# A graph network kernel: batch 0's GAT stage and the edge tables put between the steps of layer 0's last chunk, score broadcasts made by transposes, and a new order of steps

## The reference

```python
def _L1_gnn_ref(h, adj_matrix, W, a):          # the "GAT" layer
    Wh = jnp.einsum('bnf,fo->bno', h, W)
    a1, a2 = (a[:Fout, 0], a[Fout:, 0])
    s1 = Wh @ a1
    s2 = Wh @ a2
    e = s1[:, :, None] + s2[:, None, :]
    e = jnp.where(e >= 0, e, ALPHA * e)
    e = jnp.where(adj_matrix[None] == 0, -jnp.inf, e)
    attention = jax.nn.softmax(e, axis=-1)
    h_prime = jnp.einsum('bij,bjo->bio', attention, Wh)
    return h_prime
...
    h = jnp.maximum(_layernorm(x, axis=-1), 0.0)
    x = x + _L0_gnn_ref(h, adj, ...)            # 8 Euler steps: h + dt*(0.5*alpha*(adj@h - h) + h@w_eff - h + x0)
    h = jnp.maximum(_layernorm(x, axis=-1), 0.0)
    x = x + _L1_gnn_ref(h, adj, ...)
    h = jnp.maximum(_layernorm(x, axis=-1), 0.0)
    x = x + _L2_gnn_ref(h, ..., adj, src, dst)  # attention over 256 edges, 4 heads: leaky_relu(Xq[src] + Xq[dst]) . a,
                                                # + log(adj[src, dst]), softmax by source node, sum of values, W_out
    h = jnp.maximum(_layernorm(x, axis=-1), 0.0)
    x = x + _L3_gnn_ref(h, adj, adj, ...)       # Chebyshev step with 2L/lambda_max - I, masked attention of 4 heads, FFN
```

## Time and profile before

| | us |
|---|---|
| median of 3 runs | 1332.32 (1326.53, 1332.32, 1336.32) |
| the profiled execution, its own time | 1326.59 |
| its span in the profile | 1324.8 |
| mean granted clock of PE, share of full | 0.957 |
| PE busy | 1176.4 (89%) |
| DVE busy, ACT busy, POOL busy | 784.3 (59%), 762.5 (58%), 473.9 (36%) |
| 16 DMA engines, mean share, moved | 83.68 MB, 63 GB/s |

### The profile page before, as it was taken

How to read it: one execution, slowest core, us unless ns; L and a number is a source line. 1 busy time by engine, 2 the same in 40 slices (tenths; PEclk the granted TensorE clock), 3 DMA queues, 4 the chain that set the end, 5 groups by cost and what they waited for, 6 DMA issues and landing times. The chain is left out here.

```text
span 1324.8 us, 24887 instructions
## 1 busy us (share of the span) xinstructions
PE 1176.4 (89%) x7613; PEld 920.3 (69%) x7613; DVE 784.3 (59%) x2837; ACT 762.5 (58%) x1612; POOL 473.9 (36%) x578
## 2 busy tenths in 40 slices
PE   4979999999999547899999999999999999999763
PEld 3658878888889435677776777777777677766542
DVE  6623213213332234677888888888888888866652
ACT  4213324234211023487888788788888878885770
POOL 4203003003125022335346445644644654552423
PEclk7989999999999768999999999999999999998996
DMA  4001020020200100223323423432432342343311
GB/s 117 16 17 33 24 65 8 25 72 1 64 9 9 32 8 17 66 68 99 90 71 97 112 64 87 111 89 62 111 95 62 97 111 65 86 104 86 96 51 31
DMA packets 123748, 83.68 MB, mean 63 GB/s; under 512 B 13216, under 2 KB 106784, under 8 KB 123680
## 3 DMA queue, kind: packets, MB, share of 16 engines
q1 hardware_dynamic: 123680, 82.82, 23.8%
HBM read 28.25 MB, written 20.97 MB: 37 GB/s over the span
## 5 line engine op out<-in xcount | busy, mean ns | idle before, releaser
L1726 DVE CUSTOM_DVE_ANT_0 att_Ts<-bank,mask_att 128x512 f32<-128x512 f32 x256 | 173.5, 685 | 71.7 <-PE bank L1811 70.2
L1521 ACT ACTIVATE att_Es<-att_Ts,att_small 128x512 f32<-128x512 f32 x256 | 184.6, 721 | 39.0 <-DVE att_small L1726 38.1
L1951 PE MATMUL bank<-ident,att_Es 128*128 128x128 f32 x1024 | 157.2, 276 | 23.3 <-ACT att_PTs L1529 22.7
L1529 ACT COPY att_PTs<-bank 128x512 f32<-128x512 f32 x256 | 147.5, 576 | 32.1 <-PE bank L1951 31.3
L1951 PEld LDWEIGHTS bank<-ident,att_Es 128*128 128x128 f32 x1024 | 118.5, 142 | 67.3 <-issue 29.8
L1811 PE MATMUL bank<-K_parts,Q_parts 128*128 128x512 f32 x256 | 125.6, 500 | 9.0 <-DMA K_parts<-k_lo 8.8
L290 POOL TENSOR_SCALAR l_rs<-l_mv 128x4 f32<-128x4 f32 x16 | 6.9, 431 | 251.3 <-DVE l_mv L470 251.1
L1456 POOL TENSOR_SCALAR gat_Vs<-gat_Ts,gat_small 128x512 f32<-128x512 f32 x64 | 62.4, 989 | 54.4 <-DVE gat_small L1603 54.4
L484 DVE TENSOR_TENSOR P_row<-bank,l_bias 128x512 f32<-128x512 f32 x32 | 22.1, 691 | 99.2 <-PE bank L855 77.8
L845 PE MATMUL bank<-G,x0T 128*128 128x128 f32 x384 | 75.0, 277 | 1.2 <-DVE U2T L479 1.0
L845 PE MATMUL bank<-G,U1T 128*128 128x128 f32 x384 | 74.4, 275 | 0.0
(11 more groups left out here) (307 smaller groups left out, 3101.2 us busy)
## 6 DMA issues: line engine op xcount, KB each, us to landing
Q_parts<-q_hi SPq DMA_DIRECT2D x128, 64.0 KB, 2.0
Q_parts<-q_lo SPq DMA_DIRECT2D x128, 64.0 KB, 2.0
K_parts<-k_hi SPq DMA_DIRECT2D x128, 64.0 KB, 2.0
K_parts<-k_lo SPq DMA_DIRECT2D x128, 64.0 KB, 2.0
l_x<-in_x SPq DMA_DIRECT2D x16, 256.0 KB, 2.9
P2T<-in_x SPq DMA_DIRECT2D x16, 256.0 KB, 4.2
x_after_l<-P2T SPq DMA_DIRECT2D x16, 256.0 KB, 2.3
gat_xin<-x_after_l SPq DMA_DIRECT2D x16, 256.0 KB, 2.9
```

What stands on the lines that cost most here:

```text
L1521: nc.scalar.activation(att_E[:, j % RING_E, :], att_T[:, j % RING_T, :], ACT.Exp, scale=-1.0, bias=att_small[:, 0, j:j + 1], accum_out=att ...
L1529: nc.scalar.copy(att_PT[:, i // NT, :, cols(i % NT)], c2[:].rearrange("p (s q) -> p s q", q=P)).then_inc(sem("att_pt"), 1)
L1726: nc.vector.tensor_tensor_reduce(att_T[:, j % RING_T, :], [c0, c1][j % 2][:], k.mask_att[:, j % NT, :], -QK_SCALE, HUGE, ALU.add, ALU.min, ...
L1951: mm = nc.tensor.transpose(c2[:, cols(s)], att_E[:, i % RING_E, cols(s)], k.ident[:])
```

## The change

The GAT stage moves out of `build_layers` into functions of its own (`gat_stage`, `gat_memory`), whose semaphores are kept over the barrier. Both blocks use it. Batch 0's whole GAT stage is issued by the front block, between the steps of the last chunk: `with_gat(lev, t)` says on each engine what follows which step. `pick_adj` moves from behind the last level to (0,3), where it reads `edge_pick` itself; `pick_s` is gone. The loads of the edge lists move to the first chunk and `same_src`, `src_rows` to the second. On POOL `gat_rstd(0)` stands ahead of the `edge_pick` tables. The semaphore clear becomes 12 instructions.

In both blocks the score vectors are folded in elsewhere: `gat_wh` multiplies by `W1ga`, 130 columns, of which the last two are the scores; `gat_s1`, `gat_s1_out`, `gat_a2b` are gone, `gat_s2` becomes 4 transposes of a broadcast column. `gat_wh_out` is two copies, one per half. The destination's edge scores come from `edge_lcol`, which moves ahead, a small copy `edge_lc` on DVE, and 8 transposes of broadcast columns (`edge_lb0/1`) where 4 matmuls with `head_a` stood. The three order tables are new: in the loop `cheb_g` is ahead of `gat_turn`, `ffn_turn` ahead of `att_turn3`, and `store_out` last on SP.

```diff
@@ -89,37 +95,36 @@
-        gat_a = sb("gat_a", [P, 2])
-        gat_a2b = sb("gat_a2b", [P, P])
-        head_a = sb("head_a", [P, H, P])
+        W1ga = sb("w_W1ga", [P, D + 2])
+        W["W1g"] = W1ga[:, 0:D]
         head_a4 = sb("head_a4", [P, H])
...
+        k["gat"] = gat_memory(nc)
+        k["gat_steps"] = gat_stage(nc, k, kept_sem)
         build_front(nc, k)
...
+        def gat_wh_out(n, half):
+            ready(act, "gat_wh", n, half + 1, 2)
+            freed(act, "gat_pv", n)
+            nc.scalar.copy(WhA[:, 2 * half:2 * half + 2, :],
+                           [a1, a0][half][:, 0:2 * (D + 2)].rearrange("p (t d) -> p t d", d=D + 2)
+                           ).then_inc(sem("gat_whs"), 1)
...
+        def gat_wh(n):
+            ready(pe, "gat_hT", n)
+            freed(pe, "gat_eT", n, NT)
+            w = D + 2
+            for t in range(NT):
+                mm = nc.tensor.matmul([a1, a0][t // 2][:, t % 2 * w:t % 2 * w + w], hTA[:, cols(t)], k.W1ga[:],
+                                      start=True, stop=True)
+                if t % 2:
+                    mm.then_inc(sem("gat_wh"), 1)
+
+        def gat_s2(n):
+            ready(pe, "gat_whs", n, 2, 2)
+            for t in range(NT):
+                mm = nc.tensor.transpose(a1[:, cols(t)], wh2[:, t, :].broadcast_to([P, P]), k.ident[:])
+            mm.then_inc(sem("gat_s2"), 1)
+
...
+                if ch == 0:
+                    for dst, src in edge_loads:
+                        load(dst, src, "edge_loaded")
                 if ch == NCH - 1:
                     sp.wait_ge(sem("u_ready"), 2 * B)
-                    for dst, src in edge_loads:
-                        load(dst, src, "edge_loaded")
+                    for t in range(NT):
+                        sp.wait_ge(kept_sem(f"l0_stored{t}"), 16)
+                    gat["load_x"](0)
...
+            def edge_tables():
+                nc.gpsimd.iota(node_row[:], [[1, N]], base=0, channel_multiplier=0,
+                               allow_small_or_imprecise_dtypes=True).then_inc(sem("node_numbers"), 1)
+                pool.wait_ge(sem("edge_f"), 2)
+                pool.wait_ge(sem("node_numbers"), 2)
+                for e in range(ET):
+                    nc.gpsimd.tensor_scalar(k.same_src[:, e, :], edge_f[:, 0, :], edge_c[:, 0, e:e + 1], None,
+                                            ALU.is_equal).then_inc(sem("rows"), 1)
+                    nc.gpsimd.tensor_scalar(k.src_rows[:, e, :], node_row[:], edge_c[:, 0, e:e + 1], None,
+                                            ALU.is_equal).then_inc(sem("rows"), 1)
...
+                if ch == 1:
+                    edge_tables()
...
+            gat["gat_rstd"](0)
...
+            for half in range(2):
+                for t in range(NT):
+                    nc.gpsimd.tensor_scalar(k.edge_pick[:, t, half * E:half * E + E], edge_f[:, half, :],
+                                            node_col[:, t:t + 1], None, ALU.is_equal).then_inc(sem("pick"), 1)
...
+            for t in range(NT):
+                gat[f"gat_low{t}"](0)
+            pool.wait_ge(sem("adj_picked"), ET)
...
+                elif (lev, t) == (1, 0):
+                    gat["gat_hT"](0)
+                elif (lev, t) == (1, 1):
+                    gat["gat_wh_out0"](0)
+                    gat["gat_wh_out1"](0)
...
+                elif (lev, t) == (2, 0):
+                    for q in range(NT):
+                        gat[f"gat_exp{q}"](0)
+                elif (lev, t) == (2, 1):
+                    gat["gat_eT0"](0)
+                    gat["gat_eT1"](0)
+                elif (lev, t) == (2, 2):
+                    gat["gat_eT2"](0)
+                    gat["gat_eT3"](0)
...
-                    nc.vector.tensor_scalar(k.head_a[r, h, :], k.ones[r, :], acol[r, :], None, ALU.mult
-                                            ).then_inc(sem("head_a"), 1)
...
+                if (lev, t) == (0, 3):
+                    gat["gat_stats"](0)
+                    gat["gat_aggr"](0)
+                elif (lev, t) == (1, 0):
+                    gat["gat_apply"](0)
+                    edge_weights()
...
+                        if ch == NCH - 1:
+                            for q in range(NT):
+                                gat[f"gat_scores{q}"](0)
+                            gat["gat_row1"](0)
+                            gat["gat_row2"](0)
+                            gat["gat_row3"](0)
+            gat["gat_rinv"](0)
+            gat["gat_x2a"](0)
+            gat["gat_x2b"](0)
...
+                if (lev, t) == (0, 3):
+                    pick_adj()
+                elif (lev, t) == (1, 0):
+                    gat["gat_turn"](0)
+                elif (lev, t) == (1, 1):
+                    gat["gat_wh"](0)
...
+                elif (lev, t) == (2, 1):
+                    gat["gat_eturn0"](0)
+                    gat["gat_eturn1"](0)
+                elif (lev, t) == (2, 2):
+                    gat["gat_eturn2"](0)
+                    gat["gat_eturn3"](0)
+                elif (lev, t) == (2, 3):
+                    gat["gat_pv0"](0)
+                    gat["gat_pv1"](0)
...
             def pick_adj():
 
                 pe.wait_ge(sem("pick"), NT)
-                pe.wait_ge(sem("lap"), NT)
+                pe.wait_ge(sem("lap"), 2 * NT)
                 for e in range(ET):
                     for t in range(NT):
-                        mm = nc.tensor.matmul(bank[4 + e][:], pick_s[:, t, cols(e)], adj[:, t, :],
+                        mm = nc.tensor.matmul(bank[4 + e][:], k.edge_pick[:, t, cols(e)].bitcast(F32), adj[:, t, :],
                                               start=(t == 0), stop=(t == NT - 1))
                     mm.then_inc(sem("adj_picked"), 1)
...
-        cheb_prop0 cheb_prop1 att_turn1 att_score4 gat_turn cheb_g att_turn2 att_score5 gat_wh gat_s1 att_turn3
-        ffn_turn gat_s2 ffn_up0 att_score6 ffn_up1 att_turn4 att_score7 ffn_down0 ffn_down1 cheb_x1turn
...
+        cheb_prop0 cheb_prop1 att_turn1 att_score4 cheb_g gat_turn att_turn2 att_score5 gat_wh ffn_turn att_turn3
+        gat_s2 ffn_up0 att_score6 ffn_up1 att_turn4 att_score7 ffn_down0 ffn_down1 cheb_x1turn att_turn5 att_score8
+        edge_gather0 att_turn6 att_score9 edge_gather1 cheb_q edge_x att_turn7 att_score10 gat_eturn0 edge_lcol
+        att_turn8 edge_lb0 edge_lb1 att_score11 gat_eturn1 att_turn9 att_score12 cheb_k gat_eturn2 gat_eturn3 edge_v
...
-        load_x store_out+ load_ffn edge_store+ stack1+ stack3+ store_v+ load_v cheb_res stack0 stack2
+        load_x load_ffn stack1+ stack3+ store_v+ edge_store+ cheb_res load_v stack0 stack2 store_out
...
+            def edge_lc(n):
+                ready(dve, "edge_lcol", n)
+                freed(dve, "edge_lb", n, 2)
+                nc.vector.tensor_copy(edge_small[:, 5, :], b0[:, 0:ET * H]).then_inc(sem("edge_lc"), 1)
...
+            def edge_lcol(n):
                 ready(pe, "edge_z", n)
-                for h in (2 * q, 2 * q + 1):
-                    mm = one([b0, b1][q][:, (h % 2) * E:(h % 2) * E + E], k.head_a[:, h, :], zT[:])
-                mm.then_inc(sem("edge_lb"), 1)
-
-            def edge_lcol(n):
-                ready(pe, "edge_max", n, ET * H, ET * H)
                 for e in range(ET):
                     mm = one(b0[:, e * H:e * H + H], zT[:, cols(e)], k.head_a4[:])
                 mm.then_inc(sem("edge_lcol"), 1)
+
+            def edge_lb(n, q):
+                ready(pe, "edge_lc", n)
+                for h in (2 * q, 2 * q + 1):
+                    for e in range(ET):
+                        c = e * H + h
+                        mm = nc.tensor.transpose([b0, b1][q][:, (h % 2) * E + e * P:(h % 2) * E + (e + 1) * P],
+                                                 edge_small[:, 5, c:c + 1].broadcast_to([P, P]), k.ident[:])
+                mm.then_inc(sem("edge_lb"), 1)
```

767 lines of the change are left out of this document (396 added, 371 removed).

## The result

The changed kernel takes 1312.12 us (median of four runs, 1311.06 to 1314.35), the kernel before 1331.05 (four runs): a ratio of 0.986 with an interval of 0.983 to 0.990. It is faster by 1.4%, 19 us in the medians. I had said 1294, with a range of 1276 to 1311. Its profiled execution took 1312.6 us with a span of 1310.8, which is 14.0 us less than the span of before.

A forecast was written before the change was run, and what follows sets the result against it. PE was taken to bound the loop. Gains of 16 (front block), 1.3 (its start), 5 (fill), 15 (loop) and 1 (drain) sum to 38 us: 1326.6 becomes 1288.3, as a median 1294, range 1276 to 1311.

The forecast's parts named there:

- The stall ahead of `pick_adj`: Front block: PE waits 10.4 us for four `edge_pick` tables that POOL makes behind `gat_rstd(0)`.
- the early 1.3 us: Early front block: DVE's `gat_a2b` and `head_a` mostly go, so PE's wait for DVE's list shrinks by 1.3 us.
- The clears: Border between the blocks: 11 more semaphore clears on POOL cost 0.5 us, bounds 0 and 2.5.
- Rival 3: Front block: the GAT stage does not overlap and levels stretch; 16 us gain becomes 3, giving 1307; chance 0.08.
- the loop is bound by PE: Loop: PE, busy 45.36 of 47.30 us, sets the period; it shrinks by 1.5 us to 45.8, gaining 15 us.
- 0.81 + 0.5 + 1.0 = 2.3: Loop: PE work lost per iteration, 0.81 us from `gat_s1`, 0.5 from `gat_s2`, 1.0 from the edge scores.
- The floor under `ffn_turn`: Loop: `ffn_turn` needs POOL's `n2_b`, whose chain is not shortened, so it moves only 0.81 us ahead, not 1.28.
- Rival 2: Loop: removed matmuls turn into waits for DVE or ACT, the new order gives nothing; 1312 us; chance 0.14.
- The fill: Fill, batches 1 to 5: the same edits gain 5 us, bounds −2 and 10.
- The drain: Drain, with no GAT stage and one edge stage: 1 us gained.
- rival 5: DVE's `edge_lc` waits for `edge_lcol`, delaying masks, exponentials and PE's turns 4.5 us a round; 1354 us; chance 0.05.
- rival 4: The clock falls where transposes stand in a row, 3 us in each of 13 rounds; 1333 us; chance 0.03.

The follow-up runs named there:

- e1: The changed kernel with POOL's eight `edge_pick` tables ahead of `gat_rstd(0)`: 1295.82 us, ratio 0.973 to the kernel before.
- e2: The changed kernel with all kept semaphores taken first, so that one instruction clears the rest: 1305.65 us, ratio 0.982 to the kernel before.
- e16: The kernel before, unchanged, profiled a second time: 1328.09 us (one run).
- e14: The changed kernel with `cheb_k`'s matmul issued twice, 0.86 us more PE work per iteration: 1314.49 us, ratio 0.992 to the kernel before.
- e15: The changed kernel with `gat_wh`'s matmuls issued twice, 0.9 us more PE work per iteration: 1314.05 us, ratio 0.990 to the kernel before.
- e6: The changed kernel with `edge_lb` made again by four fp32 matmuls with `head_a`, in its new place: 1316.13 us, ratio 0.991 to the kernel before.
- e9: The changed kernel with the loop lists of before on PE, DVE, ACT, POOL and SP, adapted to the new operations: 1315.92 us, ratio 0.991 to the kernel before.
- e13: The changed kernel with POOL's `n2_b` adding the bias to the first of four node tiles only: 1307.74 us, ratio 0.985 to the kernel before.
- e7: The changed kernel with added matmuls that nobody reads at four PE waits in the fill: 1308.12 us, ratio 0.984 to the kernel before.
- e4: The changed kernel with `att_rv` back ahead of `cheb_aggr`, `ffn_final` and `gat_x2` in DVE's loop list: 1310.99 us, ratio 0.986 to the kernel before.
- e5: The changed kernel with the loop lists of before on PE, DVE, ACT and POOL, but SP's new list: 1350.12 us, ratio 1.017 to the kernel before.

## Why the prediction was wrong

**The front block: right in mechanism, one term too small.** 14.6 us came, 17.3 were forecast. The stall ahead of `pick_adj` (9.76 for 10.4), its second price in the clock (1.56 for 1.4), `gat_turn`'s wait (1.81 for 1.8) and the early 1.3 us (1.14: PE starts at 71.10 where it was at 72.24) are right, and e1 showed the stall to be POOL's order. The clears are the mis-sized term: 1.6 us (e2), for 0.5. Of the 2.7 us that are missing they are 1.1, and another 0.3 are at the border; 0.5 are that `pick_adj` starts at 406.96 and not at 407.8 − 1.3, and 0.8 lie between there and the x2 operations (61.7 us for 60.9). Rival 3, that the stage would not overlap, is out.

The two marks move with the granted clock as well. The stretch from 380 to 390 us, with PE at work in it, first before and then in the changed kernel:

```profile
380.00:390.00 10.00, 9.01 (x81) 8.93 (x81) 2.49 (x8) 0.62 (x1) 0.56 (x1) 1.00 0.15 28
380.00:390.00 10.00, 10.00 (x63) 10.00 (x62) 1.80 (x7) 0.62 (x1) 0.00 (x0) 0.66 0.01 2
```

So of the 1.14 us that PE was early at 71.10 only 0.4 are left where level 0 ends, at 397.0. The kernel before has such a dip in its second profile too (e16, 0.67), and there the first edge statistics come at 488.98 where the first profile had 488.07.

**The loop: the step that failed** is "the loop is bound by PE", read from PE's 96% share, and with it the sum "0.81 + 0.5 + 1.0 = 2.3" carried to the period. The period fell by 0.3 us. Adding 0.9 us of PE work did nothing (e14, e15), taking 1.0 us back cost 0.25 (e6), and with the old lists the lighter work was no faster than the heavier (e9 against before). When work is taken out, waits take its place, partly where only the weight loads show them, and so PE's busy share stayed at 95%.

**The floor under `ffn_turn`** was the right rival mechanism with a wrong number: I kept the n2 chain's end at 13.45 us behind `att_pv`, and it moved to 13.99, as `att_rv` and `ffn_wo` stand later (`ffn_wo` starts 5.08 us behind `att_pv`, and 4.59 before). Of the 0.83 us that I gave to that stretch, `ffn_up`'s start gained 0.22: 15.41 against 15.63. But even without the floor the gain is 0.25 (e13). Rival 2, that removed matmuls turn into waits and the loop gives nothing, is what happened there, except that the order itself is worth 0.5 us per period against the old one with the same operations (e9). That its number, 1312, is the measured median to 0.1 us is luck: it had 2 us gained in the fill, which lost, 1 in the drain, which gave 3.7, and 17.3 in the front block.

**The fill** was forecast as 5 us gained "since the same edits act"; it lost 5.2 in the profile and 2.2 by the means of several. The same step failed: PE's work was taken as what the time is made of, and here PE waits for chains to begin with. How much of the loss is the granted clock's is open (0.82 on the mean against 0.93 and 0.91), but raising it did not win the time back (e7).

**The drain** gave 3.7 us for 1: from batch 12's to batch 13's `att_pv` it is 42.9 us for 47.3. But in the second profile of before (e16) that distance is 45.3 us, with 201.8 us from batch 11's `att_pv` to the end (201.5 in the first), and in the unchanged drains of e1, e2 and e4 that stretch is 197.9, 195.1 and 194.9. No run here took it apart.

**Slower by the `edge_lc` wait** (rival 5) did not come: PE waits 0.3 us for it at most. **The clock under transposes** (rival 4) did not either: the granted clock is 1.00 in the period above, with eight and four transposes more in it. Two of its figures do not come from the rows: `att_score11` stands between `edge_lb` and `gat_eturn1`, so that the row named is 8 and, with `att_turn8` ahead of it, 12 (1000.57 to 1001.83), and the 1.2 us until the clock is back stand in no row, while the front block's prices were 1.4 forecast and 1.56 measured. By the rule of the Trainium skill's "TensorE: Matmul & The Clock Gate", Part 4, that a transpose does not count as PE work in the same way, the clock could have been lower; here no stretch of the steady loop shows one, but no run has transposes alone either.

**What stays open** is what sets the period of about 46.9 us. Cuts of 0.8 us on POOL's n2 step, 0.86 on ACT and 1.03 on DVE each gave 0.25 to 0.32 (0.20 to 0.27 against the mean of 46.92), a cut of 1.0 on PE 0.25, and additions on PE nothing; no two cuts were tried at once. A ring that goes over all four engines, with a share of each, would act so, but no run shows it.

## What to carry to other kernels

A busy share of 95 or 96% does not show a bound: before the price of removed work is carried to the period, read whether the engine's next steps have their inputs earlier as well, in the weight loads' waits too, and best add a little work there, which in this kernel's steady loop cost nothing at 95% (e14, e15). When a stage is moved in between others, look through every in-order queue that it passes: here one line on POOL (e1) was worth 12 to 16 us, not far from the whole change's 19. Lists of several queues belong together: `store_out` last on SP is harmless with the new DVE list and costs 3.2 us per period with the old one (e5 against e9).

## What the runs showed that I had not expected

- One semaphore clear more or less counts: 12 for 1 cost 1.6 us between the blocks (3.65 to 2.04 us of wait).
- The same lists gave a fill of 114.2 to 119.2 us in seven profiles, at three places that go with the granted clock there; the mean clock of whole executions of e2 ran from 0.954 (1309.6 us) to 0.975 (1301.3 us). On this kernel a single profile can't price a change in the fill to better than 5 us.
- PE's timeline can show no wait where PE lost time: the load of `edge_x` waits 0.9 us, and PE's rows show only that `cheb_q` ahead of it is 0.24 us longer to the next start.
